# Linear-attention layer with softmax heads: scores as float32r products in 64-row tiles, and a whole key tile per head through VectorE

## The chip, the cores and the metric

One NeuronCore of one Trainium2 chip. The metric is the device time of one launch in microseconds, lower is better. A core has TensorE (PE, with its weight loads shown as PEld), VectorE (DVE), ScalarE (ACT), GpSimd (POOL) and SyncE (SP), which here issues nearly all DMAs.

## What is computed

For 2 sequences of 2,048 tokens of width 512: a layer norm, softmax attention mixed with a read of a fixed memory matrix, a residual, a second layer norm, a product with rounding to 8-bit floats, and a residual. Cut to what matters:

```python
# x: (2, 2048, 512), 4 query groups x 8 heads of width 16, K and V have 8 heads
q, k, v = xn @ Wq.T, xn @ Wk.T, xn @ Wv.T
scores = einsum('bsqhd,bthd->bqhst', qh, kh) / sqrt(16)
a_dot  = einsum('bqhst,bthd->bsqhd', softmax(scores), vh)
sigma  = elu(q);  a_mem = sigma @ memory / (sigma @ memory_norm)
x = x + a_dot * (1 - w) + a_mem * w
x = x + (float8(layernorm(x) / s) * s) @ (w8 * weight_scale).T
```

The exponentials are most of it: 2 x 32 x 2048 x 2048, about 268 million.

## The kernel before

**Two stages.** First all 8 chunks of 512 tokens are normalised, turned and projected (`chunk` on each engine). q, k, v and sigma go to DRAM. Each 128x512 strip of q or k is split into three bf16 parts: ScalarE copies the strip to part 0, VectorE subtracts it (L1018), ScalarE copies the rest to part 1 (L609), VectorE makes part 2 (L931).

**The attention stage** runs 64 "heads", one for each chunk of queries and each of 8 key heads; a head covers its 4 query groups, so 2,048 queries against 2,048 keys, in 16 key tiles of 128 keys. Its unit of work is half a key tile: 128 keys x 1,024 queries, two PSUM banks. Per unit TensorE makes two strips of scores (`scores`, `strip`, L753), ScalarE takes the exponential of 128x1024 (L641), and once both halves of a key tile are there TensorE weighs the values (`weigh_v`, L775), accumulating over key tiles in PSUM bank 6 or 7 (`acc[par]`, by the head's parity). The units use three PSUM slots of two banks, so TensorE may be three units ahead of ScalarE and no more.

A strip is 128 keys x 512 queries. It contracts 99 rows of bf16: six products of parts, 16 rows each, and 3 rows for a per-query bound that keeps the exponent in range. It is made as four products of 32 keys in four column tiles of 32, which run side by side (the rows read `99*32 99x512`). The weighing is in fp32, again four column tiles (`128*32`).

**VectorE's share.** Of the last key tile (15), half the queries do not go through ScalarE: `late_strip` writes each of two strips into the accumulator that the other parity is not using, VectorE takes it (L1081, 692 ns) and the next strip may then be written; `late_exps` computes the exponential as a polynomial (L1083 to L1097). So a head has 31 units on ScalarE and one half tile on VectorE. TensorE runs the late strips at units 5 and 7 and weighs that half at unit 24.

**Other work in the stage**, by VectorE in program order. Even heads: `late_exps`, `add_memory` (memory read, first half), `round_to_float8` of one token tile of the chunk before, `add_memory` (second half), `add_head` (turns the accumulator by tokens, divides, adds to the residual). Odd heads: `late_exps`, `ffn_out`, `add_head`. TensorE does the memory products in even heads and the second-layer products in odd heads, at listed units. `add_head` waits until the head's last weighing is done, which comes at unit 1 of the next head, and TensorE may not write late strips into that accumulator before `add_head` has read it.

**SP** runs its list in order: for each head an operand load (`load_block`: six loads of q parts, three of k, one of v, one of the bound), in even heads a load of sigma, and after each odd head's load the four DMA transposes of `turn_tile`, which wait for `round_to_float8` of the even head. Operand buffers are double, by parity, so a head's load can begin when the head two before it is finished.

The order on TensorE is written out by unit: `WEIGH_AT`, `LATE_AT`, `WEIGH_LATE_AT`, `MEMORY_AT`, `FFN_PRODUCT_AT` name the unit after whose scores each thing is put.

## Time and profile before

| | |
|---|---|
| median of 3 runs | 2065.89 us (2065.71 to 2066.22) |
| profiled execution: its own time | 2065.7 us |
| its span | 2064.0 us |
| PE busy | 2029.0 us, 98% |
| ACT busy | 1933.2 us, 94% |
| DVE busy | 1118.2 us, 54% |
| POOL busy | 82.3 us, 4% |
| granted TensorE clock, mean | 0.996 |
| first strip of the attention stage | at 210.96 us |
| last strip | at 2037.7 us |
| chain that ended last, by line | PE L753 43%, PE L775 43%, PE L698 6% |

How to read it: busy time is the union of an engine's instructions. A matmul's record lasts longer than it holds up the next one (a strip's record is 379 ns, and strips follow each other at about 215 ns), so a busy TensorE is not one at its peak: the distance between starts is what counts. The same holds for ScalarE: records of 1152 ns, one every 0.92 us. In the row names a shape such as `128*32` is rows x columns of the array in use.

### The profile page before, as it was taken

Reading aid. Unit: us, or ns where it says so; the run is one execution under the profiler, and the core shown is the slowest. Engines: PE = TensorE matmul, PEld = TensorE weight load, DVE = VectorE, ACT = ScalarE, POOL = GpSimd, SP = SyncE. Lnnn points to the kernel's source line nnn. Section 1 sums busy time; section 2 is a strip of 40 time slices with the busy share of each in tenths; the row PEclk is TensorE's granted clock in tenths of the full one; section 3 lists DMA queues with packets and bytes.
Section 4 is the critical chain, followed back from the end, with each engine's and each line's share of the span. In section 5 each row is a group of like instructions: output and inputs, shape, how many; then the busy total and the mean of one; then the engine's idle time right before and its main releaser. Section 6 shows DMA issues by size and latency. Waiting matters only on the chain.

```text
span 2064.0 us, 62714 instructions
## 1 busy us (share of the span) xinstructions
PE 2029.0 (98%) x27379; PEld 897.5 (43%) x27380; DVE 1118.2 (54%) x1716; ACT 1933.2 (94%) x2180; POOL 82.3 (4%) x135
## 2 busy tenths in 40 slices
PE   8999999999999999999999999999999999999996
PEld 4555443334444444444444444444444444444442
DVE  5775544555445555455554555545555445555456
ACT  4555999999999999999999999999999999999995
POOL 3322000000000000000000000000000000000000
PEclk9999999999999999999999999999999999999998
DMA  5656211111111211112121111221121211121111
GB/s 191 196 186 206 62 48 35 36 48 51 51 42 39 72 50 51 40 44 61 50 51 50 53 49 51 51 65 36 45 49 51 71 37 43 51 71 51 33 43 42
DMA packets 137558, 131.57 MB, mean 64 GB/s; under 512 B 31520, under 2 KB 113824, under 8 KB 137312
## 3 DMA queue, kind: packets, MB, share of 16 engines
q1 hardware_dynamic: 135248, 125.11, 21.8%
q8 instruction: 215, 3.52, 0.7%
q10 hardware_dynamic: 2064, 2.69, 0.4%
q14 instruction: 31, 0.25, 0.0%
HBM read 86.57 MB, written 37.49 MB: 60 GB/s over the span
## 4 chain that ended last, share of the span: by engine, by line
PE 97%; DVE 2%; ACT 1%; DMA 0%; issue 0%; ACTq 0%; POOL 0%; DVEq 0%; POOLq 0%
PE ps L753 43%; PE ps L775 43%; PE ps L698 6%; PE ps L810 1%; PE ps L796 1%; PE ps L713 1%; PE ps L667 1%; DMA mem_aug<-in_memory_norm 0%; ACT pool L641 0%; DVE ps L1018 0%; DVE pool L906 0%; DVE parts L931 0%; DVE work L1177 0%; PE ps L682 0%; PE ps L675 0%
## 5 line engine op out<-in xcount | busy, mean ns | idle before, releaser
L641 ACT ACTIVATE pool<-ps 128x1024 f32<-128x1024 f32 x1984 | 1823.8, 1152 | 8.8 <-PE ps L753 5.7
L753 PE MATMUL ps<-q_st,k_st 99*32 99x512 bf16 x16384 | 1121.2, 379 | 3.2 <-issue 3.2
L775 PE MATMUL ps<-pool,v_st 128*32 128x512 f32 (+1 forms) x8704 | 1080.0, 567 | 0.5 <-ACT pool L641 0.5
L753 PEld LDWEIGHTS ps<-q_st,k_st 99*32 99x32 bf16 x16384 | 459.7, 96 | 815.7 <-issue 500.6
L775 PEld LDWEIGHTS ps<-pool,v_st 128*32 128x32 f32 x8704 | 281.5, 110 | 206.7 <-ACT pool L641 1.4
L1102 DVE STREAM_TRANSPOSE by_token<-ps 128x512 f32<-128x512 f32 x64 | 45.9, 717 | 484.0 <-PE ps L775 484.0
L1095 DVE SCALAR_TENSOR_TENSOR parts<-parts 128x1024 f32<-128x1024 f32 x192 | 235.3, 1225 | 6.6
L1081 DVE TENSOR_SCALAR parts<-ps 128x512 f32<-128x512 f32 x128 | 88.6, 692 | 131.4 <-PE ps L753 131.4
L698 PE MATMUL ps<-pool,wqT 128*128 128x512 f32 x256 | 111.4, 592 | 0.0
L596 ACT ACTIVATE parts<-ps 128x512 bf16<-128x512 f32 x40 | 23.9, 597 | 62.5 <-PE ps L698 62.5
L1154 DVE SCALAR_TENSOR_TENSOR y_out<-ps,scalars,resid 128x512 f32 x28 | 21.0, 752 | 113.2 <-PE ps L796 113.2
L1086 DVE SCALAR_TENSOR_TENSOR parts<-parts 128x1024 f32<-128x1024 f32 x64 | 78.4, 1226 | 2.2
L1097 DVE SCALAR_TENSOR_TENSOR pool<-parts 128x1024 f32<-128x1024 f32 x64 | 78.4, 1225 | 2.2
L549 POOL TENSOR_TENSOR var_eps<-moments,eps 128x1 f32<-128x1 f32 (+1 forms) x29 | 5.6, 192 | 1815.9 <-DVE moments L1132 1771.7
L1092 DVE SCALAR_TENSOR_TENSOR parts<-parts 128x1024 f32<-128x1024 f32 x64 | 78.0, 1218 | 0.0
L698 PEld LDWEIGHTS ps<-pool,wqT 128*128 128x128 f32 x256 | 47.9, 190 | 56.9 <-issue 55.0
L1013 DVE SCALAR_TENSOR_TENSOR y_out<-work,ps 128x512 f32<-128x512 f32 x32 | 21.9, 685 | 56.7 <-ACT work L604 56.7
L1189 DVE SCALAR_TENSOR_TENSOR resid<-ps,rnorm,resid 128x128 f32 (+1 forms) x128 | 41.3, 349 | 14.2 <-DVE rnorm L1185 13.7
L1083 DVE TENSOR_SCALAR parts<-parts 128x1024 f32<-128x1024 f32 x64 | 44.4, 694 | 2.2
L1090 DVE TENSOR_SCALAR parts<-parts 128x1024 int32<-128x1024 int32 x64 | 44.4, 694 | 2.2
L796 PE MATMUL ps<-wT_ffn,xqT 128*32 128x512 bf16 x448 | 44.8, 381 | 0.0
L810 PE MATMUL ps<-mem_aug,wqT 128*32 128x129 f32 x1024 | 39.7, 273 | 0.0
(125 smaller groups left out, 740.4 us busy)
## 6 DMA issues: line engine op xcount, KB each, us to landing
q_st<-q_aug SPq DMA_DIRECT2D x384, 64.0 KB
v_st<-v_aug SPq DMA_DIRECT2D x64, 256.0 KB
q_aug<-parts SPq DMA_DIRECT2D x96, 128.0 KB
k_st<-k_aug SPq DMA_DIRECT2D x64, 192.0 KB
sigma_kept<-y_out SPq DMA_DIRECT2D x32, 256.0 KB, 3.6
k_st<-k_aug SPq DMA_DIRECT2D x64, 128.0 KB
wqT<-sigma_kept SPq DMA_DIRECT2D x32, 256.0 KB, 3.3
resid<-in_x SPq DMA_DIRECT2D x7, 1024.0 KB, 9.1
```

The costliest lines, as they stand in the source:

```text
L641: act.activation(held[:, half_u * 2 * CH:half_u * 2 * CH + 2 * CH], sc[unit % SLOTS].rearrange("p a b -> p (a b)"), ACT.Exp, scale=EXP_UNIT)\
L698: last = pe.matmul(pj[i % len(pj)], w, xnT[:, par, k, :], start=(k == 0), stop=(k == KT - 1))
L753: last = pe.matmul(dst[VW * c:VW * c + VW, :], k_st[0:AUG, par, keys:keys + VW], q_st[0:AUG, par, q * CH:q * CH + CH], start=True, stop=True)
L775: last = pe.matmul(acc[par][VW * c:VW * c + VW, :].rearrange("v (i s) -> v i s", s=VW)[:, places, :], v_st[:, par, j, :], by_place[:, c, p ...
L796: last = pe.matmul(ffn_ps[VW * c:VW * c + VW, :], xqT[:, k, VW * c:VW * c + VW], wT_ffn[:, k, :], start=(k == 0), stop=(k == KT - 1))
L810: last = pe.matmul(am[VW * c:VW * c + VW, t, :], sigma_st[:, tokens:tokens + VW], mem_aug[:, :], start=True, stop=True)
L1081: dve.tensor_scalar(late_x[:, d * CH:d * CH + CH], acc[1 - par], LOWEST, None, ALU.max).then_inc(late_taken, 1)
L1086: dve.scalar_tensor_tensor(late_x, late_z, ROUND, late_x, ALU.subtract, ALU.subtract).then_inc(late_step, 1)
L1092: dve.scalar_tensor_tensor(late_p, late_x, POWER[4], late_x, ALU.add, ALU.mult).then_inc(late_step, 1)
L1095: dve.scalar_tensor_tensor(late_p, late_p, POWER[i], late_x, ALU.add, ALU.mult).then_inc(late_step, 1)
L1097: dve.scalar_tensor_tensor(late_probs[:, LATE * CH:2 * LATE * CH], late_p, POWER[0], late_z, ALU.add, ALU.mult)\
L1102: dve.transpose(by_token[:, :, :, :].rearrange("p q t v -> p (q t v)"), acc[par]).then_inc(acc_read, 1)
```

## The change

The parts are now two 32-bit numbers: `HIGH_BITS` masks the low 12 bits away, and the rest is the difference. Their products, 3 terms of 16 rows and 2 rows of the bound, make 50 rows, which fit in half the array's rows. Operands are float32r; a strip is a single product of 50 rows by 128 keys. q strips 0 and 2 lie on partitions 0 to 49, strips 1 and 3 on partitions 64 to 113, and the keys lie on both, so that a unit's two strips stand in different row tiles of 64 and different banks.

VectorE takes all four strips of key tile 15, in two halves of `late_exps`, and does so for the next head: `late_strip(n, ...)` uses the operands of head n + 1 and writes the accumulator of that parity. Only in head 0 does ScalarE do tile 15. ScalarE thus has 30 units a head. The late strips stand at units 8 to 11 of even heads and 10 to 13 of odd ones, each waiting until the one before is taken, and the late halves are weighed at units 12 and 16 of the next head. In even heads `add_head` stands in the middle of the second half of `late_exps` (`FRONT`, `BACK`).

SP's load of a head no longer waits for the weighing two heads before but for its scores; it has eight loads of q and k and two of the bound, then v. The late strips wait for that load (`qk_loaded[1 - par]`). The splitting in the first stage is wholly VectorE's (`split_strip`); ScalarE's two copies per strip go. Several small buffers move into ones that are free in the attention stage.

```diff
+PARTS = 2
+TERMS = 3
+AUG = TERM_ROWS + PARTS
+ROW_TILE = 64
+HIGH_BITS = -2 ** 12
-LATE = 2
-LATE_AT = (5, 7)
-WEIGH_LATE_AT = (6, 24)
+LATE = QG
+LATE_AT = ((8, 9, 10, 11), (10, 11, 12, 13))
+WEIGH_LATE_AT = (12, 16)
-FFN_PRODUCT_AT = (10, 14, 18, 22)
-MEMORY_AT = (12, 26)
+FFN_PRODUCT_AT = (15, 17, 19, 21)
+MEMORY_AT = (14, 25)
...
             def load_block(g, h):
-                sp.wait_ge(pv_done, (n - 1) * ST)
-                load_qk(n, g, h, par, operands_loaded[par])
+                sp.wait_ge(scores_ready, n * UNITS + units_before(0 + 1) - 2 * UNITS)
+                load_qk(n, g, h, par, qk_loaded[par])
+                load_guard(n, par, qk_loaded[par])
+                sp.wait_ge(pv_done, (n - 1) * LATE_TILE)
                 load_v(g, h, par)
-                load_guard(n, par, operands_loaded[par])
...
             def strip(dst, par, j, q):
-                for c in range(P // VW):
-                    keys = j * P + c * VW
-                    last = pe.matmul(dst[VW * c:VW * c + VW, :], k_st[0:AUG, par, keys:keys + VW],
-                                     q_st[0:AUG, par, q * CH:q * CH + CH], start=True, stop=True)
-                return last
+                rows = slice(q % ROW_TILES * ROW_TILE, q % ROW_TILES * ROW_TILE + AUG)
+                tokens = q // ROW_TILES * CH
+                return pe.matmul(dst, k_st[rows, par, j * P:j * P + P], q_st[rows, par, tokens:tokens + CH],
+                                 start=True, stop=True)
...
             def late_strip(n, par, d):
                 if d == 0:
                     pe.wait_ge(acc_read, n + TWO_FREE)
+                    pe.wait_ge(qk_loaded[1 - par], ((n + 1) // 2 + 1) * 16 * QK_LOADS)
                 else:
-                    pe.wait_ge(late_taken, n * LATE + 1)
-                strip(acc[1 - par], par, LATE_TILE, 2 + d).then_inc(late_scores, 1)
+                    pe.wait_ge(late_taken, n * LATE + d)
+                strip(acc[1 - par], 1 - par, LATE_TILE, d).then_inc(late_scores, 1)
...
+            def split_strip(c, o):
...
+                dve.tensor_scalar(parts[:, o, 0, :].bitcast(I32), here.bitcast(I32), HIGH_BITS, None, ALU.bitwise_and)\
+                    .then_inc(high_ready, 1)
+                if o >= 1:
+                    make_sigma(c, o - 1)
+                dve.wait_ge(high_ready, i + 1)
+                dve.tensor_tensor(parts[:, o, 1, :], here, parts[:, o, 0, :], ALU.subtract).then_inc(low_ready, 1)
...
+            def even_head(n, g, hp, between):
+                take_late(n, 0)
+                late_exps(n, 0, ALL)
+                add_memory(g, hp, 0)
+                between()
+                add_memory(g, hp, 1)
+                late_exps(n, 1, FRONT)
+                add_head(n, 0, g, 2 * hp)
+                late_exps(n, 1, BACK)
+
+            def odd_head(n, g, hp, between):
+                take_late(n, 1)
+                late_exps(n, 0, ALL)
+                between()
+                late_exps(n, 1, ALL)
+                add_head(n, 1, g, 2 * hp + 1)
```

(`between` is `round_to_float8` in even heads and `ffn_out` in odd ones, and in the first 8 heads the decoding of the 8-bit weight and nothing.)

**TensorE, around the late strips of an odd head.** Before (L753 strips, four products each; L775 weighing, `32x256` the late half; L796 second-layer product):

```order
L753 MATMUL ps<-q_st,k_st 32x512 x16
L775 MATMUL ps<-pool,v_st 32x512 x4
L753 MATMUL ps<-q_st,k_st 32x512 x20
L775 MATMUL ps<-pool,v_st 32x256 x4
L753 MATMUL ps<-q_st,k_st 32x512 x8
L775 MATMUL ps<-pool,v_st 32x512 x4
L753 MATMUL ps<-q_st,k_st 32x512 x20
L775 MATMUL ps<-pool,v_st 32x512 x4
L753 MATMUL ps<-q_st,k_st 32x512 x8
```

After (L775 strips, one product each; L798 weighing; L824 second-layer product):

```order
L775 MATMUL ps<-q_st,k_st 128x512 x4
L798 MATMUL ps<-pool,v_st 32x512 x4
L775 MATMUL ps<-q_st,k_st 128x512 x6
L798 MATMUL ps<-pool,v_st 32x512 x4
L798 MATMUL ps<-pool,v_st 32x256 x4
L775 MATMUL ps<-q_st,k_st 128x512 x6
L798 MATMUL ps<-pool,v_st 32x512 x4
L775 MATMUL ps<-q_st,k_st 128x512 x2
L824 MATMUL ps<-wqT,v_tiles 32x512 x4
L775 MATMUL ps<-q_st,k_st 128x512 x2
L798 MATMUL ps<-pool,v_st 32x512 x4
```

Each row `x20` holds two units' strips and one late strip, and the two late strips are two units apart with a weighing between them. Now each row `x6` holds two units' pairs and two late strips: four late strips in four successive units, the first and second and the third and fourth with only a pair between them, the second and third with a pair, a weighing and, in odd heads, a late half.

**VectorE, even head.** Before, `late_exps` and the start of `add_memory`, of one head:

```order
L1081 TENSOR_SCALAR parts<-ps 128x512 x2
L1083 TENSOR_SCALAR parts<-parts 128x1024
L1086 SCALAR_TENSOR_TENSOR parts<-parts 128x1024
L1090 TENSOR_SCALAR parts<-parts 128x1024
L1092 SCALAR_TENSOR_TENSOR parts<-parts 128x1024
L1095 SCALAR_TENSOR_TENSOR parts<-parts 128x1024 x3
L1097 SCALAR_TENSOR_TENSOR pool<-parts 128x1024
L1185 RECIPROCAL rnorm<-ps 128x2
L1189 SCALAR_TENSOR_TENSOR resid<-ps,rnorm,resid 128x128 x2
```

After, from the second `add_memory` of an even head through the second half of `late_exps` with `add_head` (L1151 to L1160) in its middle:

```order
L1238 SCALAR_TENSOR_TENSOR resid<-ps,rnorm,resid 128x128 x2
L1129 TENSOR_SCALAR parts<-parts 128x1024
L1132 SCALAR_TENSOR_TENSOR parts<-parts 128x1024
L1136 TENSOR_SCALAR parts<-parts 128x1024
L1138 SCALAR_TENSOR_TENSOR parts<-parts 128x1024
L1142 SCALAR_TENSOR_TENSOR parts<-parts 128x1024
L1151 STREAM_TRANSPOSE v_tiles<-ps 128x512
L1153 RECIPROCAL rden<-v_tiles 128x16
L1155 TENSOR_TENSOR q_sq<-v_tiles,rden 128x256
L1160 TENSOR_TENSOR resid<-resid,q_sq 128x4x4x16
L1142 SCALAR_TENSOR_TENSOR parts<-parts 128x1024 x2
L1146 SCALAR_TENSOR_TENSOR pool<-parts 128x1024
```

The four takes and a whole half of `late_exps` stand ahead of this, and the next head's takes follow.

**SP, from the transposes of one pair of heads into the load for the next even head.** Rows ISA and REGISTER_ALU are register work. Before:

```order
L455 DMA_TRANSPOSE xqT<-xq_now 128x128 x4
L437 REGISTER_ALU
L371 ISA
L371 DMA q_st<-q_aug 16x2048 x3
L371 ISA
L371 DMA q_st<-q_aug 16x2048 x2
L371 ISA
L371 DMA q_st<-q_aug 16x2048
L377 ISA
L377 DMA k_st<-k_aug 48x4x512
L377 DMA k_st<-k_aug 32x4x512
L377 DMA k_st<-k_aug 16x4x512
```

After:

```order
L489 DMA_TRANSPOSE v_tiles<-v_tiles 128x128 x4
L470 ISA
L398 ISA
L398 DMA q_st<-q_aug 32x2x512
L398 DMA q_st<-q_aug 16x2x512
L402 ISA
L402 DMA k_st<-k_aug 16x4x512
L402 DMA k_st<-k_aug 32x4x512
L398 ISA
L398 DMA q_st<-q_aug 32x2x512
L398 DMA q_st<-q_aug 16x2x512
L402 DMA k_st<-k_aug 16x4x512
```

Behind it come one more load of k and two of the bound before the load counts as complete; the place of the load behind the transposes is the same.

## Rows read from the trace of the kernel before

**Rows 1.** Busy time by stretch: PE, PEld, DVE, ACT, POOL; clock; DMA share, GB/s

```profile
165.00:190.00 25.00, 25.00 (x98) 13.92 (x97) 14.49 (x27) 13.37 (x25) 6.41 (x7) 1.00 0.73 246
...
1000.00:1500.00 500.00, 500.00 (x7292) 214.33 (x7288) 261.92 (x384) 499.04 (x544) 6.60 (x18) 1.00 0.19 49
```

**Rows 2.** Groups by line and shape: count, busy us, mean ns, idle before

```profile
L641 ACT ACTIVATE pool<-ps 128x1024 f32<-128x1024 f32 x1984 | 1823.8, 1152 | 8.8 <-PE ps L753 5.7
L753 PE MATMUL ps<-q_st,k_st 99*32 99x512 bf16 x16384 | 1121.2, 379 | 3.2 <-issue 3.2
L775 PE MATMUL ps<-pool,v_st 128*32 128x512 f32 x7680 | 1001.5, 592 | 0.5 <-ACT pool L641 0.5
```

**Rows 3.** Timeline of VectorE: start, us; the transposes that end three heads in a row

```profile
1013.82 0.72 DVE L1102 STREAM_TRANSPOSE by_token<-ps 128x512 f32<-128x512 f32 x1 [9.41 <-PE ps L775]
...
1042.38 0.72 DVE L1102 STREAM_TRANSPOSE by_token<-ps 128x512 f32<-128x512 f32 x1 [5.45 <-PE ps L775]
...
1070.92 0.72 DVE L1102 STREAM_TRANSPOSE by_token<-ps 128x512 f32<-128x512 f32 x1 [9.42 <-PE ps L775]
```

**Rows 4.** Timeline of TensorE in the middle of a head

```profile
1007.50 1.06 PE L775 MATMUL ps<-pool,v_st 128*32 128x512 f32 x8
1008.37 1.07 PE L753 MATMUL ps<-q_st,k_st 99*32 99x512 bf16 x16
1009.23 1.07 PE L775 MATMUL ps<-pool,v_st 128*32 128x512 f32 x8
```

**Rows 5.** Timeline of TensorE, first stage: column tiles, then the whole array

```profile
34.91 0.40 PE L675 MATMUL ps<-q_sq,head_ones 128*32 128x512 bf16 x4
35.23 3.84 PE L713 MATMUL ps<-wvT,pool 128*128 128x128 f32 x32
...
35.23 0.19 PEld L713 LDWEIGHTS ps<-wvT,pool 128*128 128x128 f32 x1 [0.23 <-issue]
```

**Rows 6.** Timeline of TensorE: strips, a turn of the whole array, strips

```profile
430.18 0.60 PE L753 MATMUL ps<-q_st,k_st 99*32 99x512 bf16 x8
...
430.72 0.40 PE L821 MATMUL ps<-ident_bf,w_val 128*128 128x128 bf16 x4
...
431.04 0.62 PE L753 MATMUL ps<-q_st,k_st 99*32 99x512 bf16 x8
```

**Rows 7.** Groups by line and shape: the one product of float32r operands

```profile
L682 PE MATMUL ps<-k_sq,head_ones_r 128*128 128x512 f32 x8 | 3.8, 478 | 4.0 <-DVE norm L935 4.0
```

**Rows 8.** Timeline of VectorE from an even head into the odd one

```profile
1018.56 0.69 DVE L1081 TENSOR_SCALAR parts<-ps 128x512 f32<-128x512 f32 x1 [1.69 <-PE ps L753]
...
1019.29 0.69 DVE L1083 TENSOR_SCALAR parts<-parts 128x1024 f32<-128x1024 f32 x1
...
1023.14 3.75 DVE L1095 SCALAR_TENSOR_TENSOR parts<-parts 128x1024 f32<-128x1024 f32 x3
...
1028.06 0.16 DVE L1185 RECIPROCAL rnorm<-ps 128x2 f32<-128x2 f32 x1
...
1029.46 0.69 DVE L1130 BATCH_NORM_STATS2 stats<-resid 128x6 f32 x1 [0.30 <-issue]
...
1034.40 0.69 DVE L1149 TENSOR_TENSOR xq_now<-work 128x512 bf16<-128x512 f32 x1 [0.15 <-DVE work L1146]
...
1044.06 0.43 DVE L1111 TENSOR_TENSOR resid<-resid,head_out 128x256 f32 x1 [0.21 <-DVE head_out L1106]
...
1060.75 0.75 DVE L1154 SCALAR_TENSOR_TENSOR y_out<-ps,scalars,resid 128x512 f32 x1 [4.04 <-PE ps L796]
```

**Rows 9.** Timeline of SP's queue: issuing an operand load, and the transposes

```profile
1013.97 2.82 SPq L371 DMA_DIRECT2D q_st<-q_aug  x6
...
1035.20 5.78 SPq L455 DMA_TRANSPOSE xqT<-xq_now  x4
```

**Rows 10.** DMA issues of the page: size, us from issue to landing

```profile
out<-y_out SPq DMA_DIRECT2D x4, 256.0 KB, 2.0
```

405 lines of the change are left out of this document (213 added, 192 removed).

## Prediction, made before the change was run

> **What bounds the kernel now.** I read the table of stretches first. In the first stage TensorE is busy without a break and nothing else is near it; in the attention stage TensorE shows 500.00 of 500 us and ScalarE 499.04, VectorE 261.92 [rows 1]. So two engines are at their limit together and VectorE has room. The timeline gives the period: the transposes that end three heads in a row stand 57.10 us apart for a pair, 28.55 us a head [rows 3]. ScalarE makes 544 units in 500 us, one in 0.92 us, and 31 of them are 28.5 us. TensorE needs, for a key tile, 0.86 us for four strips (0.215 each) and 0.86 us for the weighing [rows 4], 16 times 1.72 us, and with late strips counted in and about 0.86 us of memory or second-layer products, 28.4 us. Either alone gives nearly the period. VectorE's transposes wait 9.41 and 5.45 us for TensorE [rows 3]: that idle time is what the change wants to fill.
>
> **What goes.** ScalarE loses one unit of 31: 0.92 us a head. If it alone set the pace, a head would take 27.6 us.
>
> **TensorE's new strips.** The one float32r product in the trace is recorded once per product, at 478 ns [rows 7], while an fp32 product is recorded twice (7,680 rows of L775 for full tiles, 592 ns [rows 2]). So it does run in one pass. That a pair in two row tiles runs side by side no row shows; the four column tiles do, so I take it. But each strip now needs its own 128-column load of 32-bit weights. Such loads are followed by a product every 0.115 us (32 products in 3.84 us [rows 5]); bf16 ones every 0.06 us (four in 0.40 [rows 6]); the bounds are 0.06 and the 0.19 us of a 32-bit load's own record [rows 5]. I take 0.11, the nearest in kind. Changing between column tiles and another shape costs 0.10 to 0.11 us each way (L675 to L713 0.32 us where a strip needs 0.215; L753 to L821 and back alike [rows 5, 6]). A key tile is then: load 0.11, four strips starting 0.11 apart and the last running 0.215, together 0.65, change 0.10, weighing 0.86: 1.61 us against 1.72. A head: 15 tiles 24.1, four late strips 0.9, two late halves 0.86, other products 0.86, their changes of shape about 0.5: **27.2 us**, 0.907 a unit. TensorE is relieved by little, and still as slow as ScalarE.
>
> **The late strips.** All four go through one bank, so strip and take alternate: load 0.11, strip 0.38 (record of [rows 2]), hand-over 0.05 (L1083 starts 0.04 after the take that it waits for [rows 8]), take 0.69, hand-over 0.05: 1.28 us. Behind a late strip TensorE has only a pair of 0.43 to do in two of the three gaps, and what is queued behind the waiting strip is every following score. It stands still 0.85 us twice a head: **1.7 us a head**, where before a weighing filled the gap. In the third gap a pair, a weighing and changes take 1.72 (2.15 in odd heads with the late half). The four takes last 2 x 1.28 + 1.72 + 0.73 = 5.0 us, and 5.4 in odd heads.
>
> **VectorE's loop.** From [rows 8]: `late_exps` of 1,024 queries is 1019.29 to 1028.06, 8.77 us, of which `FRONT` ends at 1023.14 + 1.25, 5.1, and `BACK` is 3.67. The memory half is 1.4 (1.1 without its 0.30 of idle), the rounding 1029.46 to 1035.09, 5.63. `add_head` is 1042.38 to 1044.49, 2.1 [rows 3, 8]. `ffn_out` 0.75. From the first take of an even head to that of the odd one: 5.0 + 8.77 + 1.4 + 5.63 + 1.1 + 5.1 + 2.1 + 3.67 = 32.8. From there to the next even head: 5.4 + 8.77 + 0.75 + 8.77 + 2.1 = 25.8. Together **58.6 us a pair**, already more than today's 57.1. The room of [rows 1] is spent, a fifth of it on waiting in the takes.
>
> **SP's queue.** The first late strip of an odd head needs the operands of the next even head, and that load stands behind the transposes, which wait for the rounding. From the even head's first take: rounding done at 20.8, transposes issued by 26.7 (5.78 us [rows 9]), ten loads at 0.47 us (six in 2.82 [rows 9]) by 31.4, landed 2.0 us later (256 KB [rows 10]; between 0.5 and 4), strip 0.54: **33.9 us**, 1.1 later than VectorE would be there. Before, nothing needed this load until the next head began.
>
> **The sum.** Even to odd first take is 32 units, odd to even 28. TensorE could do them in 32 x 0.907 + 1.7 = 30.7 and 28 x 0.907 + 1.7 = 27.1. The later counts in each: 33.9 by SP, 27.1 by TensorE, 61.0 a pair, 3.9 more than today. 28 pairs so: +109. The first 4 pairs have no transposes, so 32.8 + 27.1 = 59.9, +2.8 each: +11. Head 0 has one more unit on ScalarE than before (0.9) and the last no late strips (-1.7). First stage: ScalarE, busy 13.37 of 25 us, loses its two copies a strip, and VectorE, busy 14.49, masks instead of subtracting twice; TensorE at 25.00 covers both [rows 1]. The stores grow from 384 to 512 KB a strip (three parts of 2 bytes, two of 4) at a DMA share of 0.73 that leaves room. I put it at nothing; if that cover failed, 8 chunks of a microsecond or two. Together +119 on the profiled execution's 2065.7 us: **2185 us**. That execution is 0.2 us from the median.
>
> **A rule that speaks against the change.** Loads overlap running products at the same rows here: L753's weights come while L775 streams, which is why strips follow at 0.215 [rows 4]. The Trainium skill (TensorE: Matmul & The Clock Gate, "The mechanism") says that a load overlaps products in flight only where the row group differs. By that the third strip's load would wait for the first, 0.11 more a tile, and TensorE would need 28.8 us a head: 62.5 a pair and 2233 us. The rows of column tiles don't bear it out, and no row shows row tiles.
>
> **Rivals.** (1) **Row tiles serve nothing, or every change of shape empties the array.** If a pair runs one after the other, four strips cost 0.97 instead of 0.65; if the array empties first, each change costs the record's tail more, 379 - 215 = 0.16 us, twice a tile. Either is 0.33 a tile, 5 us a head: 32.1 on TensorE, 1.07 a unit, 35.9 + 31.7 = 67.6 a pair, 10.5 x 32 more: **2402 us**. For it: nothing in the trace has 64 rows. Against: changes that exist cost 0.10, no more than an exposed load [rows 5, 6]. The Trainium skill (TensorEngine Tiling, "Key Properties") says that changing the tiling mode drains TensorE; by that this case would hold, but the changes in this trace disagree, for column tiles at least.
> (2) **The other side: faster.** ScalarE stays the bound and VectorE's loop fits under it. It needs a pair in 55.3 us; the price is one unit of 0.92 a head, 59 us: **2007 us**. The point is the gaps: VectorE's work without them is 8 takes of 0.73 and the rest, 54.0 a pair; if gaps in the takes cost under 1.3 us a pair instead of 4.6 and the load arrives in time, it holds. For: DVE busy 15 us a head now and 10.1 more is 25.1, well under 27.6. Against: bank and order, which no engine can go round.
> (3) **The loads hurt less.** If loads of weights cost 0.06 and SP's landing is quick, VectorE's loop alone remains: 58.6 a pair, 1.5 more than today, **2114 us**. This is the low end of the forecast.
> (4) **It nets out**: VectorE's loop is 2.5% shorter than summed and equals today's 57.1: no change.
>
> **Chances.** A measurement here tells 0.2%, 4 us, from no change. Forecast with its bounds (2110 to 2260, (3) and the load rule within it) 0.60; rival (1) 0.18, reached in part where only one direction empties the array (about 2290); rival (2) 0.17; rival (4) and its near sides 0.05. So faster 0.18, same 0.03, slower 0.79. The range leaves out most of rival (2) and the upper half of rival (1): 2040 to 2340.
>
> **What the profile after would show.** Right: ScalarE falls under 95% in the stage with gaps once or twice a head behind the late strips; first takes of pairs near 61 us apart; takes 1.3 apart in two gaps; VectorE about 85% busy, hardly waiting for `pv_done`; late strip 0 of odd heads released by a DMA, 1.61 us a tile in the middle of a head. Wrong, if tiles take 1.9 (rival 1), if ScalarE runs at 0.92 throughout (rival 2), or if VectorE waits for TensorE at its transposes as today. A loss in the first stage would be wrong too: the first strip should stay near 211 us.

## The result, and the profile after

The change made the kernel much slower: **2546.59 us** median of 4 runs (2527.85 to 2565.66) against 2065.8 us. The ratio is 1.2327, 95% interval 1.2235 to 1.2419. The forecast was 2185 us with a range up to 2340: the sign was right, the size a quarter of what came (119 us against 481).

| | before | after |
|---|---|---|
| profiled execution: its own time | 2065.7 us | 2548.51 us |
| its span | 2064.0 us | 2546.7 us |
| PE busy | 2029.0 us, 98% | 2290.3 us, 90% |
| ACT busy | 1933.2 us, 94% | 1884.9 us, 74% |
| DVE busy | 1118.2 us, 54% | 1714.0 us, 67% |
| granted TensorE clock, mean | 0.996 | 0.891 |
| first strip of the attention stage | 210.96 us | 213.24 us |
| us a head, mean | 28.54 | 36.05 |

A granted clock of 0.891 over 2546.7 us means 2 x 0.109 x 2546.7, about 555 us, at half speed (1.2 GHz instead of 2.4), since its records show 1.0 or 0.5 and nothing between. Before it was 18 us: 3.4 us at the start of the attention stage, right behind a stop of TensorE between the two stages, and the rest behind the attention stage:

```profile
210.96 3.84 PE L753 MATMUL ps<-q_st,k_st 99*32 99x512 bf16 x40 [3.19 <-issue]
...
211.60:215.00 3.40, 3.40 (x36) 1.31 (x32) 0.00 (x0) 3.38 (x4) 0.00 (x0) 0.51 0.44 119
```

(TensorE's timeline and a stretch of the kernel before; in a stretch the number ahead of the last two is the granted clock, then come the DMA engines' share and GB/s.)

From the page of the kernel after: busy times, the clock in 40 slices, the chain of waits, and the costliest groups.

```profile
PE 2290.3 (90%) x15075; PEld 752.6 (30%) x15084; DVE 1714.0 (67%) x2328; ACT 1884.9 (74%) x2038; POOL 78.5 (3%) x133
...
PEclk9999999898887888888889978988988898888899
...
PE 49%; SPq 17%; DVE 15%; DMA 10%; issue 5%; DVEq 1%; POOL 1%; ACT 0%; ACTq 0%; POOLq 0%
...
L656 ACT ACTIVATE pool<-ps 128x1024 f32<-128x1024 f32 x1922 | 1816.0, 1074 | 497.3 <-PE ps L775 492.7
...
L775 PE MATMUL ps<-q_st,k_st 50*128 50x512 f32 x4096 | 973.0, 508 | 222.6 <-DMA q_st<-guard 164.7
...
L1121 DVE TENSOR_SCALAR parts<-ps 128x512 f32<-128x512 f32 x252 | 174.2, 691 | 580.9 <-PE ps L775 580.9
...
L1151 DVE STREAM_TRANSPOSE v_tiles<-ps 128x512 f32<-128x512 f32 x64 | 45.5, 711 | 13.8 <-PE ps L798 13.8
```

ScalarE's idle time ahead of its exponentials has gone from 8.8 us [rows 2] to 497.3. The chain of waits now runs over SP's queue for 17% and over a DMA for 10%: the last piece of an operand load (`q_st<-guard`). VectorE no longer waits at its transposes (13.8 us in all, one wait alone was 9.41 before [rows 3]) but ahead of its takes, 580.9 us. The stage by stretches, to be held against [rows 1]:

```profile
1000.00:1500.00 500.00, 446.07 (x3070) 136.19 (x3070) 342.33 (x440) 385.78 (x408) 5.12 (x14) 0.88 0.24 48
```

Nobody is full: TensorE 446 of 500 us, ScalarE 386, VectorE 342, the clock 0.88.

One even head and the start of the odd one, after, TensorE's timeline (the first late strip of each is in the row with the wait for `q_st<-guard`, the last piece of the load):

```profile
1211.88 1.06 PE L798 MATMUL ps<-pool,v_st 128*32 128x512 f32 x8
1214.72 0.70 PE L775 MATMUL ps<-q_st,k_st 50*128 50x512 f32 x3 [1.78 <-DMA q_st<-guard]
1215.97 0.73 PE L775 MATMUL ps<-q_st,k_st 50*128 50x512 f32 x3 [0.55 <-DVE parts L1121]
...
1220.52 2.79 PE L798 MATMUL ps<-pool,v_st 128*32 128x512 f32 x16
1223.24 1.17 PE L775 MATMUL ps<-q_st,k_st 50*128 50x512 f32 x4
...
1226.44 1.50 PE L798 MATMUL ps<-pool,v_st 128*32 128x512 f32 x16
1227.86 0.73 PE L775 MATMUL ps<-q_st,k_st 50*128 50x512 f32 x4
...
1229.52 0.73 PE L775 MATMUL ps<-q_st,k_st 50*128 50x512 f32 x4
1230.18 1.06 PE L798 MATMUL ps<-pool,v_st 128*32 128x512 f32 x8
1231.18 0.73 PE L775 MATMUL ps<-q_st,k_st 50*128 50x512 f32 x4
...
1252.73 1.19 PE L775 MATMUL ps<-q_st,k_st 50*128 50x512 f32 x3 [3.42 <-DMA q_st<-guard]
```

SP's queue over the same time, to be held against [rows 9]:

```profile
1204.49 1.32 SPq L398 DMA_DIRECT2D q_st<-q_aug  x2
...
1209.60 1.49 SPq L423 DMA_DIRECT2D q_st<-guard  x2
...
1236.87 5.53 SPq L489 DMA_TRANSPOSE v_tiles<-v_tiles  x4
1242.68 1.34 SPq L398 DMA_DIRECT2D q_st<-q_aug  x2
...
1247.82 1.49 SPq L423 DMA_DIRECT2D q_st<-guard  x2
```

And the same time in stretches:

```profile
1204.00:1211.00 7.00, 7.00 (x48) 1.99 (x46) 5.31 (x7) 7.00 (x9) 0.00 (x0) 1.00 0.67 132
1211.00:1214.70 3.70, 1.95 (x16) 0.54 (x13) 0.00 (x0) 3.15 (x4) 0.00 (x0) 1.00 0.97 145
1214.70:1220.00 5.30, 4.37 (x20) 1.74 (x20) 2.07 (x3) 2.99 (x3) 0.00 (x0) 0.75 0.00 0
1220.00:1223.00 3.00, 3.00 (x19) 0.59 (x16) 2.61 (x3) 1.11 (x2) 0.00 (x0) 0.50 0.00 0
1226.00:1229.00 3.00, 3.00 (x32) 0.94 (x30) 2.90 (x4) 2.56 (x4) 0.00 (x0) 1.00 0.00 0
```

Read them in order. The ten issues of the load take from 1204.49 to 1211.09, 6.6 us; the DMA engines are then at a share of 0.97 with only 145 GB/s, and the load is there when TensorE goes on at 1214.72, 3.6 us after the last issue. TensorE has stood still 1.78 us by then. Between the takes it stands still again (0.55 us at 1215.97). The clock falls to 0.50 and is back at 1.00 by 1226: a whole and a half weighing take 2.72 us at 1220.52 (to the strip at 1223.24) and 1.42 at 1226.44. In the odd head the load stands behind the transposes, its last issue ends at 1249.31, and TensorE waits 3.42 us.

VectorE's timeline gives the links between the two heads: the first take, the end of the rounding, the odd head's first take.

```profile
1215.22 0.69 DVE L1121 TENSOR_SCALAR parts<-ps 128x512 f32<-128x512 f32 x1 [5.53 <-PE ps L775]
...
1236.06 0.69 DVE L1198 TENSOR_TENSOR v_tiles<-work 128x512 bf16<-128x512 f32 x1 [0.15 <-DVE work L1195]
...
1253.53 0.69 DVE L1121 TENSOR_SCALAR parts<-ps 128x512 f32<-128x512 f32 x1 [5.21 <-PE ps L775]
```

**The arithmetic of a pair.** Means over heads 12 to 59, from ScalarE's and VectorE's timelines (a head runs from its first exponential to the next head's): even heads last 34.94 us with the first take 9.61 after the head's first exponential; odd ones 39.13 with the first take at 13.95. So from even to odd first take there are 39.3 us (forecast 33.9), and back 34.8 (27.1): 74.1 a pair against 61.0. Before it was 57.1.

### The profile page after: what moved, and what is told of

It is laid out like the page before. It is cut to its first block, busy times and chain, and to the rows that moved or that the text cites. A ratio compares the mean times of both kernels' runs of the same rounds, so it can differ in the third digit from the quotient of the medians.

```text
span 2546.7 us, 39353 instructions
## 1 busy us (share of the span) xinstructions
PE 2290.3 (90%) x15075; PEld 752.6 (30%) x15084; DVE 1714.0 (67%) x2328; ACT 1884.9 (74%) x2038; POOL 78.5 (3%) x133
## 4 chain that ended last, share of the span: by engine, by line
PE 49%; SPq 17%; DVE 15%; DMA 10%; issue 5%; DVEq 1%; POOL 1%; ACT 0%; ACTq 0%; POOLq 0%
PE ps L798 22%; PE ps L775 19%; DMA q_st<-guard 10%; SPq L398 6%; PE ps L717 5%; SPq L402 5%; SPq L489 4%; DVE parts L1121 4%; DVE parts L1142 3%; SPq L423 2%; PE ps L824 2%; DVE parts L1132 1%; DVE parts L1138 1%; PE ps L732 1%; DVE parts L1129 1%
## 5 line engine op out<-in xcount | busy, mean ns | idle before, releaser
L656 ACT ACTIVATE pool<-ps 128x1024 f32<-128x1024 f32 x1922 | 1816.0, 1074 | 497.3 <-PE ps L775 492.7
L798 PE MATMUL ps<-pool,v_st 128*32 128x512 f32 x8696 | 1183.3, 631 | 0.6 <-ACT pool L656 0.6
L775 PE MATMUL ps<-q_st,k_st 50*128 50x512 f32 x4096 | 973.0, 508 | 222.6 <-DMA q_st<-guard 164.7
L775 PEld LDWEIGHTS ps<-q_st,k_st 50*128 50x128 f32 x4096 | 402.2, 200 | 1174.3 <-ACT pool L656 620.2
L1121 DVE TENSOR_SCALAR parts<-ps 128x512 f32<-128x512 f32 x252 | 174.2, 691 | 580.9 <-PE ps L775 580.9
L1142 DVE SCALAR_TENSOR_TENSOR parts<-parts 128x1024 f32<-128x1024 f32 x378 | 462.8, 1224 | 11.8
L798 PEld LDWEIGHTS ps<-pool,v_st 128*32 128x32 f32 x8696 | 195.8, 114 | 439.1 <-issue 437.3
L1132 DVE SCALAR_TENSOR_TENSOR parts<-parts 128x1024 f32<-128x1024 f32 x126 | 154.4, 1225 | 4.3
L1146 DVE SCALAR_TENSOR_TENSOR pool<-parts 128x1024 f32<-128x1024 f32 x126 | 154.3, 1225 | 4.3
L1138 DVE SCALAR_TENSOR_TENSOR parts<-parts 128x1024 f32<-128x1024 f32 x126 | 153.4, 1218 | 0.0
L1136 DVE TENSOR_SCALAR parts<-parts 128x1024 int32<-128x1024 int32 x126 | 87.4, 694 | 4.3
L974 DVE TENSOR_SCALAR parts<-ps 128x512 int32<-128x512 int32 x40 | 27.6, 690 | 57.3 <-ACT work L626 41.5
L1151 DVE STREAM_TRANSPOSE v_tiles<-ps 128x512 f32<-128x512 f32 x64 | 45.5, 711 | 13.8 <-PE ps L798 13.8
L824 PE MATMUL ps<-wqT,v_tiles 128*32 128x512 bf16 x448 | 47.6, 415 | 0.0
```

The source lines that it names most:

```text
L656: act.activation(held[:, half_u * 2 * CH:half_u * 2 * CH + 2 * CH], sc[unit % SLOTS].rearrange("p a b -> p (a b)"), ACT.Exp, scale=EXP_UNIT)\
L775: return pe.matmul(dst, k_st[rows, par, j * P:j * P + P], q_st[rows, par, tokens:tokens + CH], start=True, stop=True)
L798: last = pe.matmul(acc[par][VW * c:VW * c + VW, :].rearrange("v (i s) -> v i s", s=VW)[:, places, :], v_st[:, par, j, :], by_place[:, c, p ...
L1121: dve.tensor_scalar(late_x[:, d * CH:d * CH + CH], acc[1 - par], LOWEST, None, ALU.max).then_inc(late_taken, 1)
L1132: dve.scalar_tensor_tensor(x, late_z, ROUND, x, ALU.subtract, ALU.subtract).then_inc(late_step, 1)
L1138: dve.scalar_tensor_tensor(late_p, x, POWER[4], x, ALU.add, ALU.mult).then_inc(late_step, 1)
```

## The experiments

Two theories stood at the start. **A**: the late strips, which wait for the next head's operands, stop TensorE; the stop and a half clock behind it are what the forecast lacked. **B**: the new form of scores, or the takes themselves, cost more than was summed. Times are medians, ratios go against runs of the kernel before on the same chip. Where a time stands without a ratio it is one run.

### 1. Own operands for the late strips

```diff
-                    pe.wait_ge(qk_loaded[1 - par], ((n + 1) // 2 + 1) * 16 * QK_LOADS)
-                strip(acc[1 - par], 1 - par, LATE_TILE, d).then_inc(late_scores, 1)
+                strip(acc[1 - par], par, LATE_TILE, d).then_inc(late_scores, 1)
```

> The changed kernel with its late strips made from the running head's own operands, so that they no longer wait for the load of the next head (the values of key tile 15 then belong to the wrong head; all instructions and their number stay). Theory A, the late load stops TensorE and the stop brings the clock down: without the wait the granted clock stays at 1.0 nearly throughout, a pair of heads goes back to about 60 us by VectorE's loop, 30 a head, and the time to about 2150 (2110 to 2220). Rival B, the waits between late strips and takes alone bring the clock down: low clock in most heads still, 34 us a head or more, over 2350.

Measured: **2216.55 us**, ratio 1.0729 (1.0711 to 1.0747), clock 0.992. The first takes of even heads come at 7.69 us, of odd ones at 9.88; 30.05 and 31.70 us a head, 61.7 a pair. Of the 12.3 us a pair that this gives back, 6.0 are the first takes' lateness (9.61 - 7.69 and 13.95 - 9.88) and 6.3 come behind the first take, where TensorE now runs at full clock. Theory A holds: 330 of the 481 us lost hang on this wait, with all that follows from it. From even to odd first take there are 32.2 us, which is VectorE's loop (forecast 32.8), and back 29.5, where TensorE was forecast at 27.1.

```profile
1000.00:1500.00 500.00, 478.58 (x3628) 149.02 (x3625) 401.42 (x518) 455.21 (x485) 5.85 (x16) 1.00 0.31 60
```

(Stretch of the kernel with own operands.) VectorE is at 80%, the clock at 1.00.

### 2. Work in the place of the stop

```diff
                 if d == 0:
                     pe.wait_ge(acc_read, n + TWO_FREE)
+                    for _ in range(12):
+                        strip(acc[1 - par], par, LATE_TILE, 0)
                     pe.wait_ge(qk_loaded[1 - par], ((n + 1) // 2 + 1) * 16 * QK_LOADS)
```

> The changed kernel with 12 extra strips into the still free accumulator before the wait for the load, so that TensorE works through most of that wait (2.6 us at 2.4 GHz) and the result stays. It separates the price of the wait from that of the clock. Theory A: the clock stays up in most heads and only the wait remains: between 31 and 34 us a head, 2230 to 2400. Rival B (takes alone bring it down): the time stays at 2500 or above.

Measured: 2546.95 us, clock 0.929. A miss: about 200 us at half clock are gone and the time has not moved. The timelines tell why it settles nothing: twelve strips are 2.7 us, and they run in each head whether the load has landed or not. In the first odd heads, where it lands in time, the first take moved from 9.5 to 12.25 us. What the clock gave back, the filling took.

### 3. and 4. The new scores without VectorE's new share

Everything of VectorE's share, the units (31 on ScalarE) and the places of insertions as in the kernel before; and the same with all 32 units on ScalarE.

```diff
-LATE = QG
-LATE_AT = ((8, 9, 10, 11), (10, 11, 12, 13))
-WEIGH_LATE_AT = (12, 16)
-FFN_PRODUCT_AT = (15, 17, 19, 21)
-MEMORY_AT = (14, 25)
+LATE = 2
+LATE_AT = (5, 7)
+WEIGH_LATE_AT = (6, 24)
+FFN_PRODUCT_AT = (10, 14, 18, 22)
+MEMORY_AT = (12, 26)
```

> The scores part alone: float32r strips in row tiles, the new split and loads, but the late half tile as before the change (two late strips at units 5 and 7 from the head's own operands, 31 units on ScalarE). If the new strips are as cheap as the 1.65 us a tile in the trace of the change at full clock say, TensorE is relieved below ScalarE's 31 x 0.905 to 0.92 us and the head takes 28.1 to 28.5: 2035 to 2062, at or a little under the kernel before, clock 1.0. If the strips or the loads are what costs (rival C), it stays above 2150.

> The scores part alone with no late strips at all: ScalarE does all 32 units of a head, VectorE's exponentials go. By ScalarE's pace 32 x 0.905 to 0.92 = 29.0 to 29.4 us a head, 2095 to 2125, clock 1.0, and TensorE waits for ScalarE in every unit. If TensorE with the new strips were the slower one, it would be more, and 1.65 us a tile would be wrong.

Measured: **2118.75 us**, ratio 1.0257 (1.0240 to 1.0274), and 2119.66 us. The first is a miss: 29.25 us a head instead of at most 28.5, at a clock of 0.994. The second came as expected, at 29.33 a head, and that is nearly ScalarE's own pace: its units follow each other at 0.905 us but at two places a head, and 32 of them are 29.0. With 31 units ScalarE would need 28.1 us, 1.2 less than the 29.25 measured, so there it is not ScalarE that sets the pace. TensorE is busy without a gap, and its timeline shows where it loses (31 units; L774 strips, L796 weighing, L817 second-layer product):

```profile
1012.15 0.50 PE L774 MATMUL ps<-q_st,k_st 50*128 50x512 f32 x2
1012.58 0.40 PE L817 MATMUL ps<-wqT,v_tiles 128*32 128x512 bf16 x4
1012.91 0.49 PE L774 MATMUL ps<-q_st,k_st 50*128 50x512 f32 x2
1013.34 1.06 PE L796 MATMUL ps<-pool,v_st 128*32 128x512 f32 x8
1014.33 0.73 PE L774 MATMUL ps<-q_st,k_st 50*128 50x512 f32 x4
1015.00 1.06 PE L796 MATMUL ps<-pool,v_st 128*32 128x512 f32 x8
```

Four strips in a row take 0.67 us. Cut in two by a product, they take 0.43 + 0.33 + 0.43 = 1.19, so an insertion (a second-layer product, four column tiles side by side, 0.22 us by itself in the kernel before) costs 0.52. In the kernel before, all of these were column tiles of 32, and the same insertion stands in the same place (TensorE's timeline):

```profile
1002.53 0.63 PE L753 MATMUL ps<-q_st,k_st 99*32 99x512 bf16 x8
1002.97 0.42 PE L796 MATMUL ps<-wT_ffn,xqT 128*32 128x512 bf16 x4
1003.19 0.63 PE L753 MATMUL ps<-q_st,k_st 99*32 99x512 bf16 x8
1003.62 1.06 PE L775 MATMUL ps<-pool,v_st 128*32 128x512 f32 x8
```

There it makes 1.09 us of 0.86 [rows 4]: 0.23, its own time.

### 5. Insertions behind weighings

```diff
-WEIGH_LATE_AT = (6, 24)
-FFN_PRODUCT_AT = (10, 14, 18, 22)
-MEMORY_AT = (12, 26)
+WEIGH_LATE_AT = (7, 25)
+FFN_PRODUCT_AT = (11, 15, 19, 23)
+MEMORY_AT = (13, 27)
```

> The score part alone, as in the experiment before it, but the late halves, the memory products and the second-layer products are moved from places between two pairs of strips to places right behind a weighing (units 7 and 25, 13 and 27, 11, 15, 19 and 23). Theory A (TensorE sets the 29.25 us a head of the score part alone, because every insertion splits four strips into two and two, which costs 0.20 us more than the insertion itself): a head becomes ScalarE's 31 units of 0.905, 28.1 us, and the time is 2040 to 2055 us, under the kernel before. Theory B (something else sets 29.25 us, such as the hand-over between ScalarE and TensorE over three slots): no change, 2110 to 2125 us.

Measured: **2067.99 us** (11 runs), ratio 1.0009 (1.0000 to 1.0018): 28.49 us a head. Of the 53 us that experiment 3 lost, 51 come back, by order alone. The diagnosis holds; the number expected was too good by 13 us, since ScalarE, now without a pause of its own, still takes 1.23 us instead of 0.905 at unit 7 and 1.18 at unit 27 of even heads.

### 6. The transposes behind the load

```diff
                     load_block(g, h)
-                    if h % 2 == 1:
-                        turn_tile((g - 1) * TPC + h // 2)
+                    if h % 2 == 0:
+                        turn_tile((g - 1) * TPC + h // 2 - 1)
```

(Cut: the same for the heads of chunk 1, and one call behind the last load.)

> The changed kernel, with the four DMA transposes of an odd head issued behind the next even head's load instead of ahead of it. Theory A (the load that stands behind the transposes makes odd heads' late strips late, and the long stop brings the half clock): the first take of odd heads goes from 13.95 to 9.5 us after the head's first exponential, odd heads take 29.7 and even heads 31.4 us where the clock stays, 2170 to 2200 us in all; even heads' stop of 1.3 us remains and may still cost the clock in some heads, 4.3 us in each, at most 2310 us. Theory B (the clock falls for another reason than the long stops, with its 553 us at half speed as they are): 2450 us or more, with odd heads' takes early.

Measured: **2374.92 us**, ratio 1.1499 (1.1479 to 1.1519), clock 0.936. The first take of odd heads is at 9.84 us and they take 31.87. That is A's mechanism, but the time is above A's 2310: even heads take 35.50, since their stop (44 waits for the load, 60.7 us in all, 2.8 the longest) brings the half clock nearly each time, and not in some heads only. Half of the loss from the wait (172 of 330 us) hung on four transposes in the wrong place of a queue.

### 7. A lighter load

```diff
-                        sp.dma_start(k_st[rows, par, :].bitcast(F32).rearrange("r (c s) -> r c s", c=CPB),
-                                     k_src(b4, h, last - first)).then_inc(done, 16)
+                        sp.dma_start(k_st[rows, par, :].bitcast(F32).rearrange("r (c s) -> r c s", c=CPB)[:, 0:chunks, :],
+                                     k_src(b4, h, last - first)[:, 0:chunks, :]).then_inc(done, 16)
```

(`chunks` is 1 for the second row tile from head 2 on.)

> The changed kernel, but from head 2 on the load for the second row tile brings only the first quarter of the keys (0.89 instead of 1.18 MB a head, the same number of issues); the other three quarters stay as head 0 or 1 left them, so strips 1 and 3 use wrong keys there. Theory A (saturated DMA queues make the load late by its volume): it lands 1.5 to 2 us earlier, even heads' first take at 7.8 us and odd ones at 12, the half clock in fewer heads, 2300 to 2450 us. Theory B (the ten issues of 0.6 us and a fixed time to landing set it): takes as before, 2520 to 2570 us.

Measured: 2404.69 us, clock 0.933. Even heads: first take 7.98 us, 30.80 us a head. Odd: 13.18 (A had 12) and 38.31, still behind the transposes. The issues take as long as before (in even heads the last begins 5.04 us after the head's first exponential, 4.93 in the changed kernel), but in odd heads the time from the last issue's end to the late strip falls from 3.8 to 1.8 us. So what the load carries made the landing late. Bytes and number of rows fall together here, by a quarter, and which of the two it is stays open.

### 8. Both cures

The transposes behind the load, and the light load.

> Both cures of the load at once: the transposes behind the load and the light load for the second row tile (three quarters of the keys wrong there, as before). Theory A (what the changed kernel loses beyond its forecast is the late load, in odd heads by the transposes and in even ones by its volume, with the half clock that follows): no stop ahead of the late strips but 0.3 us, clock at full speed as with the running head's own operands (2216.55 us), 2205 to 2235 us. Theory B (something of the change still costs beside the load): 2260 us or more.

Measured: **2234.49 us**, clock 0.985; 30.84 and 31.63 us a head, first takes at 7.96 and 9.80. With the wait still in place, but the load on time, the kernel is within 18 us of the one without the wait. Theory B falls: what the wait costs is the lateness of the load and what follows from it. What the kernel without the wait still takes above the forecast (61.7 us a pair against 59.9) is in both kernels, and no experiment takes it apart.

### 9. Late strips two units apart

```diff
-LATE_AT = ((8, 9, 10, 11), (10, 11, 12, 13))
+LATE_AT = ((6, 8, 10, 12), (8, 10, 12, 14))
```

(on the kernel with own operands, so the last key tile's scores are those of the running head here too)

> The changed kernel with the late strips from the running head's own operands (no wait for the next load), and now two units apart (units 6, 8, 10, 12 of even heads, 8, 10, 12, 14 of odd ones), so that a pair and a weighing fill every gap. Theory A (TensorE's standing still in the takes, 1.7 us a head, is on the path where TensorE sets the pace, from odd to even head): odd to even first take 29.5 goes to 28 to 28.7 us, even to odd stays near 32.3 to 33 by VectorE, 2170 to 2205 us. Theory B (VectorE's loop sets both ways): the takes last longer, 2215 to 2240 us.

Measured: 2282.08 us, clock 0.953, outside both theories. Even heads got shorter than any with four late strips, 28.24 us. But the takes of an even head now last 6.1 us from the first to the last, VectorE comes to the odd head late, and TensorE stops at unit 10, since its second late strip may not be written before VectorE has taken the first, that of unit 8:

```profile
1009.26 0.96 PE L775 MATMUL ps<-q_st,k_st 50*128 50x512 f32 x5
1010.15 1.06 PE L797 MATMUL ps<-pool,v_st 128*32 128x512 f32 x8
1014.65 1.64 PE L775 MATMUL ps<-q_st,k_st 50*128 50x512 f32 x5 [3.44 <-DVE parts L1120]
```

No load is waited for here, and the clock falls all the same (five strips in 1.64 us, against 0.96): here the half clock follows a stop of TensorE that no load made. Odd heads take 36.27 us.

### 10. Even heads' strips two units later

```diff
-LATE_AT = ((8, 9, 10, 11), (10, 11, 12, 13))
-FFN_PRODUCT_AT = (15, 17, 19, 21)
-MEMORY_AT = (14, 25)
+LATE_AT = ((10, 11, 12, 13), (10, 11, 12, 13))
+FFN_PRODUCT_AT = (14, 18, 20, 22)
+MEMORY_AT = (14, 26)
```

(with the transposes behind the load)

> The changed kernel with the transposes behind the load, even heads' late strips two units later (10 to 13, as in odd heads) so that the load has landed, and the second-layer and memory products moved right behind weighings (14, 18, 20, 22 and 14, 26). Theory A (the load only has to be there by the time it is asked for): takes start at 9.5 to 10 us in all heads, full clock, 32.3 us from even to odd by VectorE and 29 to 31.5 us back by TensorE, which now has 30 units there, 2190 to 2275 us. Theory B (the half clock comes with any late strips of this kind): over 2330 us.

Measured: 2302.38 us, ratio 1.1136 (1.1119 to 1.1153), clock 0.961; between the theories. Even heads start their takes at 9.63 us and run at full clock, as A had it, 30.24 us each. Odd heads 34.60: VectorE's 32.7 us from first take to first take put the odd head's at 12.1, TensorE stops some 3 us for it at the second late strip, and the half clock is back. This second wait, for VectorE, had been hidden by the first. The insertions were moved too, and that shows by itself: behind the second-layer products ScalarE's steps in odd heads (units 18, 20, 22) are 0.95 us where experiment 6 has 1.27.

### 11. A smaller filling, even heads only

On the kernel with the transposes behind the load, eight strips (1.7 us) ahead of the wait in even heads.

> The changed kernel with the transposes behind the load (2374.92 us), and TensorE's stop ahead of an even head's first late strip filled with eight strips whose result nobody reads, 1.7 us of work. Nothing else about the load changes; it still lands at 9.1 to 10 us. Theory A (the stop of 1.3 to 2 us costs little by itself, and the half clock that follows it costs 4 us): even heads go from 35.5 to 31.4 to 32 us, 2250 to 2290 us, and the time at half clock falls from 307 us to under 100. Theory B (the late load itself is what even heads lose): 2365 to 2400 us.

Measured: 2341.70 us, ratio 1.1344 (1.1324 to 1.1364), clock 0.966; even heads 33.29 us instead of 35.50. A by direction, short in size: 14 of 32 even heads still lose the clock, and 158 us (2 x 0.034 x 2323.7, of the profiled execution, the fastest of the four) pass at half speed instead of under 100. And in eleven of these 14 TensorE had not stood still for more than 0.6 us at a time. Two heads of this kernel, one without and one with the half clock:

```profile
925.90:957.80 31.90, 30.78 (x244) 10.80 (x240) 21.37 (x34) 28.29 (x31) 0.73 (x2) 1.00 0.23 48
989.60:1025.70 36.10, 35.18 (x244) 11.73 (x240) 24.00 (x37) 28.23 (x31) 0.73 (x2) 0.86 0.31 70
```

The first takes of both stand 9.52 us after the first exponential, and in both TensorE's only stops over 0.1 us are two between takes (0.56 and 0.55 us, 0.56 and 0.36), so the 4.2 us between them are the clock's. The changed kernel itself has such a pair, heads 10 and 14, whose stops for the load were 1.35 and 1.33 us:

```profile
539.99:571.43 31.44, 28.99 (x232) 9.20 (x232) 21.33 (x35) 28.28 (x31) 0.74 (x2) 1.00 0.27 48
684.92:720.61 35.69, 33.45 (x232) 10.13 (x232) 23.67 (x37) 28.28 (x31) 0.74 (x2) 0.86 0.25 44
```

So a spell of 10.2 us at half clock, the length that both have, costs 4.2 to 4.3 us, three times such a stop; the shorter ones of 6.8 us in this kernel cost 2.7 (34.6 us a head against 31.9). The length of the stop alone does not decide: eight heads of the changed kernel kept the clock behind stops of 1.25 to 1.86 us, and head 56 lost it behind one of 1.29. What does, no run shows.

### 12. to 14. Can the new scores pay?

Three more orders for the kernel of experiment 5: insertions farther apart, then four units apart, then with the second late strip at unit 9 too. The second and third edit below are both against the first of the three.

```diff
-WEIGH_LATE_AT = (7, 25)
+WEIGH_LATE_AT = ((9, 21), (9, 25))
```

> The aligned score part of the experiment before, with the insertions farther apart: the first late half is weighed at unit 9 instead of 7, the second at unit 21 instead of 25 in even heads. There ScalarE stood at 0.905 us a unit but for one place early (1.23 us at unit 7 of even heads, 1.05 of odd ones) and one late (1.18 at unit 27 of even heads). Theory A (TensorE has 0.15 us a key tile to spare and loses its lead of three units where insertions come too close together): both gaps go, 28.1 to 28.3 us a head instead of 28.49, 2042 to 2056 us, under the kernel before. Theory B (the gaps only move to other units, since TensorE needs as much in all): 2062 to 2072 us.

```diff
-WEIGH_LATE_AT = ((9, 21), (9, 25))
-FFN_PRODUCT_AT = (11, 15, 19, 23)
-MEMORY_AT = (13, 27)
+WEIGH_LATE_AT = ((11, 21), (17, 29))
+FFN_PRODUCT_AT = (9, 13, 21, 25)
+MEMORY_AT = (17, 27)
```

> The aligned score part with at least four units between insertions where it can be had (first late half at unit 11 of even and 17 of odd heads, second at 21 and 29; second-layer products at 9, 13, 21, 25; memory products at 17 and 27). In the last version ScalarE's gaps stood at unit 9 (1.08 and 1.10 us instead of 0.905), 13 (1.03), 25 (1.02) and 27 (0.96). Theory A (TensorE needs 27.5 us a head and only crowding makes ScalarE wait): a head takes 28.1 to 28.25 us instead of 28.43, 2045 to 2055 us. Theory B (every insertion behind a weighing makes ScalarE wait 0.1 to 0.2 us, since TensorE cannot be more than three units ahead): 2060 to 2070 us, no better than the kernel before.

```diff
-LATE_AT = (5, 7)
-WEIGH_LATE_AT = ((9, 21), (9, 25))
-FFN_PRODUCT_AT = (11, 15, 19, 23)
-MEMORY_AT = (13, 27)
+LATE_AT = (5, 9)
+WEIGH_LATE_AT = ((13, 23), (11, 29))
+FFN_PRODUCT_AT = (13, 17, 21, 25)
+MEMORY_AT = (17, 27)
```

> As the version with four units between insertions, but the second late strip at unit 9 instead of 7, and the first late half at 13 (even) and 11 (odd), second-layer products at 13, 17, 21, 25: nothing but the first late strip is inserted among the crowded weighings at the head's start. Theory A (the lead that TensorE loses in the first eight units is what the later gaps come from): 28.1 to 28.2 us a head, 2043 to 2052 us. Theory B (as for the other version): 2060 to 2070 us.

Measured, 11 runs each: 2066.06 us, ratio 0.9995 (0.9986 to 1.0004); **2063.49**, 0.9987 (0.9978 to 0.9996); **2063.35**, 0.9985 (0.9976 to 0.9994). Theory B holds for all three: 28.43 us a head in each, wherever the insertions stand. ScalarE's steps are 0.90 to 0.91 us everywhere but at the insertions, which move with them (in the last kernel 1.08, 1.02 and 1.01 at units 13, 17 and 27 of even heads). The last two are the best versions found, 0.15% under the kernel before: less than the 0.2% that the forecast set as the bound for "no change".

## Why the prediction was wrong

**The failed step** is the price of TensorE's wait for the next head's operands. The sum gave it 1.1 us a pair (33.9 by SP where VectorE alone needed 32.8); the runs show 12.3 (74.1 a pair with the wait, 61.7 without it, experiment 1). It is 11.2 of the 13.1 us a pair by which the forecast fell short. It failed in three places.

**First part: SP's queue in odd heads.** In the head shown above, counted from the even head's first take at 1215.22, the rounding ends at 1236.75, after 21.5 us (forecast 20.8), the transposes' issue at 1242.40, 27.2 (26.7), the last issue of the load at 1249.31, 34.1 (31.4), TensorE goes on at 1252.73, 37.5 (33.4), and the odd head's first take is at 1253.53, 38.3 (33.9). The order was right to the last link. What was mis-sized is the load: 0.66 us an issue where rows of before gave 0.47, and 3.4 to 3.6 us from last issue to use where 2.0 was taken. The bound of 0.5 to 4 us was named, but the value came from four stores at the end of the kernel, where the DMA engines were at a share of 0.45. Nearer rows of the kernel before were not used: there too the engines were nearly full right behind an operand load (a share of 0.81), and the load of sigma, 256 KB and issued behind an operand load, took 3.3 us to land.

```profile
1019.00:1021.50 2.50, 2.50 (x40) 1.17 (x36) 2.40 (x4) 2.50 (x4) 0.00 (x0) 1.00 0.81 177
...
wqT<-sigma_kept SPq DMA_DIRECT2D x32, 256.0 KB, 3.3
```

The issues differ in form as well (two or three dimensions over two row tiles instead of plain rows); whether their 0.66 us comes from that, no run shows. The lighter load of experiment 7 was issued no faster.

**Second part: the even heads.** The load that an even head's late strips wait for starts 1.24 us ahead of the head and has no transposes in front; the sum had no term for it. Its last issue begins at 4.93 us, TensorE has it some 4 us later, and the late strips stand at unit 8, at 7.2 us. The wait was priced in one parity only. Shown by experiment 7 (lighter: first take 9.61 to 7.98) and 8.

**Third part: the clock.** The sum had TensorE standing still 1.7 us a head and gave it no other price. Some 555 us went by at half clock. Behind the first take a pair loses 6.3 us, half of the 12.3 that the wait costs; that these are the clock's is argued from the pairs of heads in experiment 11, where it alone costs 4.2 us. Experiments 9 and 10 show it behind stops that no load made, and experiment 11 also in heads with no stop over 0.6 us, so a long stop brings it in most heads but is not the only thing that does. The stops between takes (0.55 us, 0.95 in some odd heads) hardly brought it in experiment 1: clock 0.992. The trace of the kernel before did hold the warning, though in one place only, the stop of 3.19 us between the stages with the half clock right behind it. No row of the attention stage itself could show it, since TensorE never stopped there.

**TensorE's strips.** A key tile was forecast at 1.61 us and is 1.66 (1229.52 to 1231.18): four strips 0.66 for 0.65, weighing with both changes 1.00 for 0.96. Pairs do run side by side in row tiles. The loads of the third and fourth strip, in the rows of the first and second, begin while the first two products still run, and the tile is not 1.72 (TensorE's timeline after, 1229.71 to 1229.80):

```profile
1229.52 0.49 PE L775 MATMUL ps<-q_st,k_st 50*128 50x512 f32 x2
1229.63 0.19 PEld L775 LDWEIGHTS ps<-q_st,k_st 50*128 50x128 f32 x2
```

The Trainium skill (TensorE: Matmul & The Clock Gate, "The mechanism") says that a load overlaps products in flight only where the row group differs; this trace disagrees.

**Rival (1)** named 0.33 us more a tile: it does not hold, the two changes cost a weighing 0.14. The Trainium skill (TensorEngine Tiling (Array Packing), "Key Properties") says that changing the tiling mode drains TensorE; if it does here, it costs less than half of what rival (1) put on it.

But "changes of shape about 0.5" a head was wrong: an insertion between two pairs costs 0.3 us beyond its own time, and there are six in odd and four in even heads of experiment 3, four and one in the changed kernel. For experiment 3 it is shown that this, and not the tile, is why TensorE needed 29.25 us instead of some 28: experiment 5 has the same tile and 28.49. For the way back to even heads in experiment 1 (29.5 instead of 27.1) it explains some 1.3 us, by experiment 10's steps of 0.95 instead of 1.27; the rest is not taken apart. One reason can be read from experiment 1's timeline: between insertions the units follow each other at ScalarE's 0.905 us, not at the 0.83 (half of 1.66) that TensorE could do, so the sum's average of 0.907 over all of TensorE's work comes out too low: unit by unit the slower of the two engines counts.

**VectorE's loop.** Forecast 32.8 from even to odd; 32.2 in experiment 1, 32.7 in experiment 10, whose takes have one more late half between them. In experiment 1 the takes are 1.28 us apart in two gaps, as forecast, and 1.65 (forecast 1.72) in the third, 2.08 in odd heads (2.15); in the changed kernel, partly at half clock, they are 1.4 to 1.6 and 2.7 to 3.8. The longest estimate in the text was the best one. "About 85% busy" became 68% by the stretch above, since all waits grew; 80% in experiment 1.

**The first stage** was put at nothing; its end moved from 210.96 to 213.24 us, 2.3 us.

**What is luck.** Experiment 1's kernel, without the wait, takes 61.7 us a pair, and the forecast with the wait was 61.0; that they nearly agree is an accident. Without the wait the same terms give 59.9 (32.8 + 27.1), 1.8 too little: TensorE's way back took 2.4 more (29.5 against 27.1) and VectorE's loop 0.6 less. That 2216.55 us lies within the range does not save a forecast for the kernel that has the wait.

**Rival (2), faster,** asked for gaps in the takes under 1.3 us a pair. With no load waited for (experiment 1) they are 0.55 us each in four gaps a pair, 2.2, and more in the two others. ScalarE as the bound would have taken 27.6 us a head; in the changed kernel's order TensorE's 28 units from odd to even take 29.5.

## What to carry to other kernels

Before an engine that is hardly ever idle is made to wait, price the wait twice: once for its length, and once for the clock that may fall with it. The stages that matter may show nothing of the second; look at the places where the engine does stop, here the one between the stages. A wait that is moved from one head to the next must be priced in every parity, from first issue to landing, with the landing time of the row that is nearest in kind, not of the quickest one. And where an engine changes the shape of its work, put short pieces next to work of their own shape: here that was worth 51 us, with the same instructions.
